# Ordering five queues anew in a three-stage graph kernel, and adding the variance's constant by a two-column sum

## The reference, cut to what matters

```python
# layer 0
h = gat(x, adj, W1, a1); h = gat(h, adj, W2, a2)     # softmax over neighbours, then att @ Wh
h = layernorm(x + h, g_ln1, b_ln1)                    # norm 0
x = layernorm(h + relu(h @ w_ff1 + b_ff1) @ w_ff2 + b_ff2, g_ln2, b_ln2)     # norm 1
# layer 1: 8 heads, softmax(q k / sqrt(32)), multiplied by (adj == r) for r = 0..3, each with its own V_r
x = layernorm(x + attention(x, adj) @ Wo + bo, g1, beta1)                     # norm 2
x = layernorm(x + gelu(x @ W1 + b1) @ W2 + b2, g2, beta2)                     # norm 3
# layernorm(v) = (v - mean) * rsqrt(var + 1e-5) * g + b
```

## Time and profile before

| | |
|---|---|
| median of 3 runs | 3293.64 us (3292.21 to 3295.23) |
| profiled execution | 3299.18 us, its span 3297.4 us |
| busy over the span | PE 3113.3 us (94%), PEld 2756.9 (84%), DVE 2724.4 (83%), ACT 2203.4 (67%), POOL 1883.6 (57%) |
| DMA | 93.52 MB, 9.5% of the queues' time |
| granted TensorE clock, mean | 0.992 |

### The profile page before, as it was taken

How to read it: one execution, slowest core, us unless ns; L and a number is a source line. 1 busy time by engine, 2 the same in 40 slices (tenths; PEclk the granted TensorE clock), 3 DMA queues, 4 the chain that set the end, 5 groups by cost and what they waited for, 6 DMA issues and landing times.

```text
span 3297.4 us, 77945 instructions
## 1 busy us (share of the span) xinstructions
PE 3113.3 (94%) x27108; PEld 2756.9 (84%) x27108; DVE 2724.4 (83%) x5234; ACT 2203.4 (67%) x5706; POOL 1883.6 (57%) x1481
## 2 busy tenths in 40 slices
PE   4899999999999999999999999999999999999997
PEld 3788888888888888888888888888888888888886
DVE  5588888888888888888888888888888888888873
ACT  2577667667667667667667667667667667667663
POOL 1356566566566566566556556556556556556554
PEclk9899999999999999999999999999999999999998
DMA  4000000000000000000000000000000000000000
GB/s 129 26 24 29 25 25 29 25 25 29 25 25 29 25 25 29 25 25 29 25 25 29 25 25 29 25 25 29 25 25 29 25 26 29 24 27 29 23 14 14
DMA packets 98857, 93.52 MB, mean 28 GB/s; under 512 B 9856, under 2 KB 98048, under 8 KB 98816
## 3 DMA queue, kind: packets, MB, share of 16 engines
q1 hardware_dynamic: 98816, 92.97, 9.5%
HBM read 76.17 MB, written 16.78 MB: 28 GB/s over the span
## 4 chain that ended last, share of the span: by engine, by line
issue 43%; POOL 27%; DVE 19%; PE 7%; ACT 1%; DVEq 1%; POOLq 1%; SPq 1%; DMA 0%; ACTq 0%
POOL hid_lo L956 10%; DVE norm L762 5%; POOL res L951 5%; POOL res L948 5%; DVE masked L819 5%; POOL norm L951 3%; POOL norm L948 2%; POOL rstd L939 2%; DVE s_least L810 2%; DVE stats L751 2%; DVE masked L775 1%; DVE norm L747 1%; DVE hT_lo L767 1%; POOL rec_wide L966 1%; PE ps_f L248 1%
## 5 line engine op out<-in xcount | busy, mean ns | idle before, releaser
L956 POOL TENSOR_TENSOR hid_lo<-hid_full,hid_hi 128x512 fp32r<-128x512 f32 x512 | 837.6, 1655 | 367.4 <-ACT hid_hi L600 366.2
L939 POOL TENSOR_TENSOR rstd<-vareps,neg_half 128x2 f32<-128x2 f32 x256 | 202.7, 792 | 809.4 <-DVE vareps L757 796.4
L248 PE MATMUL ps_f<-down_w_hi,hid_hi 128*128 128x256 f32 x2048 | 594.5, 290 | 0.6 <-POOL hid_lo L956 0.4
L250 PE MATMUL ps_f<-down_w_hi,hid_lo 128*128 128x256 f32 x2048 | 570.0, 278 | 0.0
L249 PE MATMUL ps_f<-down_w_lo,hid_hi 128*128 128x256 f32 x2048 | 569.5, 278 | 0.0
L615 ACT ACTIVATE prob<-ps,s_least 128x256 f32<-128x256 f32 x1024 | 469.5, 479 | 19.4 <-DVE s_least L810 18.5
L762 DVE TENSOR_SCALAR norm<-norm,meanvar,rstd 128x256 f32<-128x256 f32 x512 | 383.6, 790 | 116.8 <-POOL rstd L939 116.4
L819 DVE SCALAR_TENSOR_TENSOR masked<-adj_in,prob 128x1024 f32<-128x1024 int32 x256 | 422.5, 1670 | 20.1 <-ACT prob L623 20.0
L248 PEld LDWEIGHTS ps_f<-down_w_hi,hid_hi 128*128 128x128 f32 x2048 | 384.8, 188 | 32.1 <-issue 25.0
L249 PEld LDWEIGHTS ps_f<-down_w_lo,hid_hi 128*128 128x128 f32 x2048 | 386.1, 189 | 3.0
L250 PEld LDWEIGHTS ps_f<-down_w_hi,hid_lo 128*128 128x128 f32 x2048 | 386.1, 189 | 0.0
(11 more groups left out here) (157 smaller groups left out, 9401.4 us busy)
## 6 DMA issues: line engine op xcount, KB each, us to landing
adj_in<-adj_keys SPq DMA_DIRECT2D x128, 256.0 KB, 2.7
xT_in<-x_features SPq DMA_DIRECT2D x64, 256.0 KB, 2.7
norm<-x_nodes SPq DMA_DIRECT2D x64, 256.0 KB, 2.7
out_nodes<-norm SPq DMA_DIRECT2D x64, 256.0 KB, 2.1
raw_up<-L_w_ff SPq DMA_DIRECT2D x1, 1024.0 KB, 5.1
raw_down<-L_w_ff SPq DMA_DIRECT2D x1, 1024.0 KB, 7.9
raw_v<-L_Wv SPq DMA_DIRECT2D x4, 256.0 KB, 7.8
raw_up<-L_W SPq DMA_DIRECT2D x1, 1024.0 KB, 9.2
```

Source lines behind the costliest of these rows:

```text
L248: nc.tensor.matmul(ps_out, left[0], right[0], start=first, stop=False)
L250: return nc.tensor.matmul(ps_out, left[1], right[0], start=False, stop=last)
L956: pool.tensor_tensor(hid[1][:, 2 * m:2 * m + 2, :], hid_full[:, 2 * m:2 * m + 2, :], value(hid[0][:, 2 * m:2 * m + 2, :]), ALU.subtract).t ...
```

## The change

Two things are changed. First, `meanvar` gets a third column, which GpSimd sets to 1e-5 once at the start (four small memsets); in place of a tensor-scalar add of the constant to the variance, VectorE sums columns 1 and 2 by a `tensor_reduce`. Second, the order of the steps in the four bodies is another. SyncE's order is as it was.

```diff
-        meanvar = [sb(f"meanvar{n}", [P, C, 2]) for n in range(4)]
+        meanvar = [sb(f"meanvar{n}", [P, C, 3]) for n in range(4)]
...
-                dve.bn_aggr(meanvar[n][:, i, :], stats[n][:, i, :]).then_inc(mv_set[n].sem, 1)
+                dve.bn_aggr(meanvar[n][:, i, 0:2], stats[n][:, i, :]).then_inc(mv_set[n].sem, 1)
             dve.wait_ge(*mv_set[n](g, 2))
-            dve.tensor_scalar(vareps[n][:].unsqueeze(2), meanvar[n][:, :, 1:2], EPS, None, ALU.add).then_inc(ve_set[n].sem, 1)
+
+            dve.tensor_reduce(vareps[n][:], meanvar[n][:, :, 1:3], AX.X, ALU.add).then_inc(ve_set[n].sem, 1)
...
+            for n in range(4):
+                pool.memset(meanvar[n][:, :, 2:3], EPS).then_inc(prep_p.sem, 1)
...
         def dve_body(dve, t, nxt, gat, ff0, att1, ff1):
...
+            if att1:
+                dve_adj_top(dve, b)
+            if ff1:
+                dve_norm_end(dve, d, 2)
...
         def pool_body(pool, t, nxt, gat, ff0, att1, ff1):
...
+            if nxt:
+                pool_gat_in(pool, e)
+            if ff1:
+                pool_hidden(pool, d, 1, 2)
+                pool_hidden(pool, d, 1, 3)
```

More of the change, by code:

```diff
@@ L489, in pe_body @@
             a, b, c, d, e = t + 1, t, t + 2, t - 1, t + 3
+            if gat:
+                pe_gat_wh1(pe, c, 0)
+            if att1:
+                pe_prob_turn(pe, b, 0, 0)
             if ff0:
@@ L496, in pe_body @@
                 pe_up(pe, a, 0, 1)
+                pe_up(pe, a, 0, 2)
+                pe_up(pe, a, 0, 3)
             if att1:
@@ L499, in pe_body @@
             if ff0:
[L500 to L504, removed]
+                pe_down(pe, a, 0, 0, 0)
             if ff1:
                 pe_turn(pe, d, 2)
+            if gat:
+                pe_gat_mix(pe, c, 0)
+                if isinstance(t, int) and t == -2:
+                    pe_setup(pe)
             if ff0:
-                pe_down(pe, a, 0, 0, 0)
-            if gat:
-                pe_gat_wh1(pe, c, 0)
+                pe_down(pe, a, 0, 0, 1)
             if att1:
@@ L545, in pe_body @@
                 pe_up(pe, d, 1, 2)
-                pe_up(pe, d, 1, 3)
             if gat:
                 pe_gat_mix(pe, c, 1)
+            if ff1:
+                pe_up(pe, d, 1, 3)
             if att1:
@@ L551, in pe_body @@
                 pe_av_one(pe, b, 1)
+                pe_av_more(pe, b, 1)
             if ff1:
@@ L634, in act_body @@
             a, b, c, d, e = t + 1, t, t + 2, t - 1, t + 3
+            if gat:
+                act_gat_pre(act, c, 0)
             if att1:
                 act_prob_turned(act, b, 0, 0)
+            if gat:
+                act_gat_wh(act, c, 0)
+            if ff0:
+                act_hidden(act, a, 0, 0)
+            if att1:
                 act_prob_turned(act, b, 0, 1)
             if ff0:
-                act_hidden(act, a, 0, 0)
                 act_hidden(act, a, 0, 1)
+            if gat:
+                act_gat_exp(act, c, 0)
+                if isinstance(t, int) and t == -2:
+                    act_setup(act)
+            if ff0:
                 act_hidden(act, a, 0, 2)
@@ L646, in act_body @@
                 act_prob(act, b, 1, 0)
-            if gat:
-                act_gat_pre(act, c, 0)
-            if att1:
                 act_prob(act, b, 1, 1)
             if gat:
[L652 to L655, removed]
+                act_gat_pre(act, c, 1)
             if att1:
@@ L875, in dve_body @@
                     dve_setup(dve)
+            if att1:
+                dve_least(dve, b, 1, 0)
+            if ff1:
+                dve_turned(dve, d, 2)
+            if att1:
+                dve_least(dve, b, 1, 1)
+                dve_rec(dve, b, 0, 0)
+                dve_reach(dve, b)
+            if gat:
+                dve_gat_wh12(dve, c, 1)
+            if att1:
+                dve_rec(dve, b, 0, 1)
+                dve_mask(dve, b, 0)
+                dve_rec(dve, b, 1, 0)
+                dve_rec(dve, b, 1, 1)
+                dve_v(dve, b, 0)
             if ff0:
                 dve_norm(dve, a, 1)
-            if gat:
-                dve_gat_wh12(dve, c, 1)
             if att1:
```

87 lines of the change are left out of this document (28 added, 59 removed).

## The result

The kernel after takes 3514.09 us in the median of 4 runs (3510.25 to 3519.24), the kernel before beside it 3294.3 (3292.21 to 3295.23): a ratio of 1.0669, 95% interval 1.0651 to 1.0688. The forecast was 3366 us and its range ended at 3425: slower was right, the size was not. Body for body the loop went from 49.52 us (mean; one of them is the earlier trace rows) to 53.26.

What follows compares the result with a forecast made beforehand. TensorE was taken as the bound: a 49.56 us body less 1.9 for three waits gives 47.7, plus 3.1 waiting for the split gives 50.8; +1.2 over some 60 bodies is +72 us, so 3366 us, range 3190 to 3425.

Steps and rivals of the forecast that it cites:

- The three old waits: TensorE's waits for norm 2's sum (0.60 us), norm 1's end (0.48) and wh's column (0.34); without them 47.7 us a body.
- the fourth wait: TensorE's wait at the reach step, 0.22 us of issue a body, not among those taken as removed.
- drain: What each TensorE wait costs beyond what it shows: some 0.16 us.
- The walk to the mix: Engine times from the end of pe_wo (time 0): TensorE at pe_gat_mix(c, 0) at 11.0 us, split asking at 9.73.
- The hold: GpSimd's operations block VectorE's split steps before pe_gat_mix(c, 0); TensorE waits 3.1 or 4.4 us, 3.1 taken; forecast's chance 0.36.
- The tie at 10.85: GpSimd's hidden part 3 asks at 10.85 us, VectorE's second high split step at 10.86; which goes first sets TensorE's wait.
- X: The end of the split on VectorE, 14.1 us after the end of pe_wo as forecast.
- rival 3: GpSimd goes before VectorE's second high split step: 4.4 us wait, 52.1 us a body, 3440 us; chance 0.16.
- The sum over two columns: VectorE's tensor_reduce taken as free of GpSimd's port: 0.17 us each, 1.2 us of VectorE won a body.
- Rival 1: The waits go and the split starts before hidden part 2: 47.7 to 48.4 us a body, 3180 to 3225 us; chance 0.28.
- Rival 2: Only one or two GpSimd operations interrupt the split: 1.7 us wait, 49.4 us a body, about 3284 us; chance 0.14.
- Rival 4: Meetings not reduced, VectorE busy 42 to 43 us but hidden, TensorE's waits still sum to 1.6: 3294 us; chance 0.06.

Runs made afterwards that it cites:

- The experiment without the shift: The kernel after, with GpSimd's addition of the shift to norm 2's result left out: 3433.65 us, ratio 1.0408.
- the filled pause: The kernel after, with 16 idle matmuls on TensorE between the turn of norm 2 and the first mix: 3398.47 us, ratio 1.0308.
- the order with the edges behind: The kernel after, with only the edges' least moved behind the split on VectorE, norm 2's end still ahead of it: 3275.04 us, ratio 0.9932.

## Why the prediction was wrong in size

**The three old waits.** Right: those at wh1, at `pe_up(a, 0, 1)` and for the end of norm 1 are gone. The body was put at 47.7 us without them, and without any wait it is 47.2. Most of that gap is the fourth wait, at the reach step, which the prediction named and left in: 0.22 us and its drain of 0.16 make 0.38, and 47.7 - 0.38 is 47.3. So the price of the three, 1.9 us, fits; the four were worth 2.3.

**The walk to the mix.** Right to within 0.5 us. Time 0 is 1536.80 in this body. TensorE was to reach the mix at 11.0 and came there at 10.9 (1551.57 - 3.86 = 1547.71); hidden part 2 was to ask at 9.4 and go at 9.55, and went at 9.03 (1545.83); the split was to start at 9.73 and started at 9.44. (Between that turn and the mix the kernel before has all four parts of `pe_down`, not three; no term hung on it.)

**The hold.** This is the first step that failed. The tie at 10.85 was given to VectorE (X = 14.1, a wait of 3.1 us). GpSimd won it:

```profile
L958 POOL TENSOR_TENSOR hid_lo<-hid_full,hid_hi x2: 1309/1388/1468, 1545.8 to 1547.3; 128x512 fp32r<-128x512 f32 x2
L726 DVE TENSOR_SCALAR att_s_hi<-score,g_rec x2: 1201/1274/1347, 1546.2 to 1547.4; 128x256 fp32r<-128x256 f32 x2
L730 DVE SCALAR_TENSOR_TENSOR att_s_lo<-score,g_rec,att_s_hi x2: 1365/1421/1477, 1548.8 to 1550.0; 128x256 fp32r<-128x256 f32 x2
```

Hidden part 3 started at 1547.26, the second high step was issued 0.11 us later, and four GpSimd operations came between the split's steps instead of three. That is rival 3's order. X was 14.7 and the wait 3.86 us, between the chosen 3.1 and the 4.4 of rival 3, since the split began 0.3 us earlier than in the walk and took 5.3 us in place of 5.7. The experiment without the shift prices an operation in the queue at 1.0 us, so the miss is most of one. The choice at the tie was a guess between two events 0.01 us apart, in a walk that was itself good to 0.5 us; both sides should have weighed about equally, and the range, which ends at 3425, leaves out rival 3's own 3440. The sum also gave the new wait no drain, though it had priced one for each old wait: 0.16 us a body, some 10 us. That the split is held at all was right: its high steps, with one input, took 1.20 and 1.35 us, its low steps, with two, 1.37 and 1.48.

**The term that was missing.** The sum had none for the clock. It had TensorE stand still for 3.1 us in each body and put what comes after at nothing, without a reason; the only clock that it had was the 1.00 of a body whose longest kind of wait is 0.60 us. The pause brought the lower level, and that cost 2.0 us a body, measured against the filled pause: half the pause's own length again. This is the larger of the two misses. Even rival 3, with its 52.1 us, would have come out 1.2 us too low.

**The sum, again.** 49.5 - 2.3 (all four old waits) + 3.86 and some 0.2 of drain + 2.0 (clock) = 53.3 us a body, measured 53.26. By 60 bodies this is some +225 us against +220 measured. With the predicted sizes it was 49.56 - 1.9 + 3.1. Of the difference of 148 us between 3514 and 3366, some 120 are the clock, some 60 the longer hold and its drain, and the lower floor gives back 30.

**The sum over two columns.** Right: 156 to 159 ns in every one of 256 places, for a taken price of 0.17 us. The Trainium skill (SBUF — State Buffer, "Who interferes with whom") says that on this chip a `tensor_reduce` never contends with GpSimd; the two traces agree. By itself it is worth 0.1%.

**What would show it.** The mix waits for L730 for 2 to 4 us: 3.86. Two waits gone: yes. L759 at 0.15 to 0.2 us always: yes. L726 or L730 at 1.3 us or more in the median: no; 353 ns for L726 and 487 for L730, with 1473 and 1478 only as the longest, since half of the splits stand in the second half of the body, where GpSimd is idle. By that sign alone one would have read the right forecast as the wrong one: it should have named the longest, or the wait. VectorE's score steps above 1 us in the opening half: the second, 1.50 us, but not the first, 0.43.

**The rivals.** Rival 1, the split ahead of hidden part 2 with nothing else late, was not reached by this order, and no run has its exact case. With the split put ahead of hidden part 2 by hand the time is 3251 us, above its 3180 to 3225, as the end of norm 2 is then late; only with the mix moved too is it 3200.82 us, inside them. That this number falls there is in part luck: a wait at the reach step is in it that the rival didn't have. Rival 2's partial hold has a like in the order with the edges behind: 1.15 us and 3275 us for its 1.7 and 3284. Rival 4 is out: VectorE is busy for some 40 us a body (375.47 of 500 us), not 42 to 43, and TensorE's waits do not sum to 1.6 us.

## What to carry to other kernels

When a step that another engine waits for is moved, list what GpSimd will have queued by then: each short VectorE step of the split's kinds (0.35 and 0.48 us) that finds GpSimd busy costs one whole GpSimd operation here (1.3 us), so that four of them in a row cost four. Wherever a forecast has TensorE stand still for several microseconds in each round, add a term for the clock behind the pause, and look for needed work, or even idle matmuls, to lie in it. Judge a new order not by how many meetings it has but by which result they delay: less VectorE time (2586 for 2724 us) went with 6.7% more time.

## What the runs showed of the hardware

- Pauses of TensorE of 3.86 and 2.86 us in a body brought the level of 1.2 GHz behind them (loop clock 0.95 and 0.96), pauses of 1.6 and 1.15 us did not (1.00). It cost 2.0 us a body at 3.86, and 51.91 - 47.2 - 2.86 - 0.2 = some 1.6 us at 2.86, where the low stretches are shorter (4.1 us a body in the mean, against 5.5). No run has a pause between 1.6 and 2.86 us.
- 16 idle matmuls in the pause made the kernel 3.3% faster than with the pause left empty (3398 for 3514 us).
- A tensor-scalar step of only 2 elements per partition is held by GpSimd like a large one (168 ns free, 943 held), a `tensor_reduce` of 4 elements is not (159 ns at most, 124 of 256 issued while GpSimd works).
- One end stays open: what would remove the 0.5 us at the reach step.
